# Attention values for all eight groups computed ahead of the group loop, row block 3 moved without DRAM, new orders

## The reference

```
xn = layernorm(x)
qkv = xn @ w_qkv.T                     # 32 query heads, 8 key and 8 value heads, 128 wide
scores = q k^T / sqrt(128), causal     # 4 query heads share one key/value head: 8 groups
attn = softmax(scores) @ v
s = attn @ w_dense.T                   # back to 512 features
g = silu(three +-1 matrix layers of xn, relu between, the last 20% of inputs times -4)
out = x + s * g
```

## Time and profile before

| | us |
|---|---|
| median of 3 runs | 915.27 (912.52 to 916.16) |
| profiled execution | 917.22 |
| its span, first to last instruction | 915.1 |
| PE busy | 896.1 (98%) |
| DVE, ACT, POOL busy | 677.7 (74%), 513.2 (56%), 463.3 (51%) |
| granted PE clock, mean | 0.997 |

### The profile page before, as it was taken

One profiled execution on the slowest core, in us unless ns is written; L12 is line 12 of the kernel. 1 busy time (PEld: TensorE's weight loads), 2 busy tenths in 40 slices (PEclk: granted clock), 3 DMA queues, 4 the chain that ended last, 5 costly groups with the idle time before them and its releaser, 6 DMA issues.

```text
span 915.1 us, 15937 instructions
## 1 busy us (share of the span) xinstructions
PE 896.1 (98%) x4272; PEld 757.4 (83%) x4272; DVE 677.7 (74%) x1163; ACT 513.2 (56%) x1077; POOL 463.3 (51%) x372
## 2 busy tenths in 40 slices
PE   7999999999999999999999999999999999999997
PEld 6878778888788878888788887888788887888886
DVE  7768767787677867788667876788677786678865
ACT  3656645665466645666356644666456663555633
POOL 5246443564346635555336634465445563355775
PEclk9999999999999999999999999999999999999999
DMA  6496655857386764865577573867549664655472
GB/s 218 121 249 192 132 115 156 241 132 152 66 239 197 155 120 115 244 165 118 103 192 222 136 155 61 243 185 153 109 127 255 157 124 86 171 151 125 103 202 86
DMA packets 204806, 143.58 MB, mean 157 GB/s; under 512 B 23152, under 2 KB 172144, under 8 KB 204784
## 3 DMA queue, kind: packets, MB, share of 16 engines
q1 hardware_dynamic: 176112, 129.68, 55.9%
q10 hardware_dynamic: 28672, 13.64, 6.9%
HBM read 63.70 MB, written 23.20 MB: 95 GB/s over the span
## 4 chain that ended last, share of the span: by engine, by line
issue 51%; POOL 30%; PE 14%; DMA 2%; SPq 1%; DVE 1%; POOLq 1%; ACT 0%; DVEq 0%
POOL pt_lo L767 21%; POOL w_lo L777 6%; POOL wd_lo L777 3%; PE ps_m L1251 3%; PE ps_s L1236 2%; PE ps_o L1119 1%; PE ps_o L1121 1%; PE ps_o L1120 1%; PE ps_m L1119 1%; PE ps_m L1120 1%; PE ps_m L1121 1%; PE ps_s L1120 1%; PE ps_s L1121 1%; PE ps_s L1119 1%; SPq L674 1%
## 5 line engine op out<-in xcount | busy, mean ns | idle before, releaser
L767 POOL TENSOR_TENSOR pt_lo<-pt_lo,pt_hi 128x512 fp32r<-128x512 f32 x248 | 326.2, 1339 | 257.6 <-ACT pt_hi L866 257.6
L959 DVE CUSTOM_DVE_ANT_0 ps_s<-ps_s,mask 128x32 f32<-128x32 f32 (+31 forms) x256 | 181.8, 716 | 93.7 <-PE ps_s L1121 92.2
L866 ACT ACTIVATE pt_hi<-pt_lo 128x512 fp32r<-128x512 f32 x288 | 172.6, 628 | 78.7 <-PE ps_o L1121 42.8
L1119 PE MATMUL ps_m<-xn_hi,w_hi 128*128 128x512 f32 (+1 forms) x388 | 152.2, 392 | 1.8 <-DVE q_lo L1067 1.8
L1121 PE MATMUL ps_m<-xn_hi,w_lo 128*128 128x512 f32 (+1 forms) x388 | 150.9, 389 | 0.0
L1120 PE MATMUL ps_m<-xn_lo,w_hi 128*128 128x512 f32 (+1 forms) x388 | 150.8, 389 | 0.0
L819 ACT ACTIVATE prob_even<-ps_s,small 128x32 f32<-128x32 f32 (+15 forms) x128 | 82.8, 648 | 99.5 <-DVE small L959 98.1
L819 ACT ACTIVATE prob_odd<-ps_s,small 128x160 f32<-128x160 f32 (+15 forms) x128 | 96.1, 754 | 63.1 <-DVE small L959 36.4
L1120 PE MATMUL ps_s<-k_lo,q_hi 128*128 128x480 f32 (+15 forms) x384 | 126.6, 330 | 0.0
L1121 PE MATMUL ps_s<-k_hi,q_lo 128*128 128x480 f32 (+15 forms) x384 | 126.5, 329 | 0.0
L1119 PE MATMUL ps_s<-k_hi,q_hi 128*128 128x480 f32 (+15 forms) x384 | 124.7, 325 | 0.0
(11 more groups left out here) (100 smaller groups left out, 1429.5 us busy)
## 6 DMA issues: line engine op xcount, KB each, us to landing
raw<-wqkv SPq DMA_DIRECT2D x48, 256.0 KB, 4.3
pt_lo<-prob_odd SPq DMA_DIRECT2D x96, 128.0 KB, 3.9
pt_lo<-prob_even SPq DMA_DIRECT2D x96, 112.0 KB, 3.2
pt_lo<-prob_odd SPq DMA_DIRECT2D x96, 96.0 KB, 2.7
raw<-wd SPq DMA_DIRECT2D x32, 256.0 KB, 4.1
inv_rows<-inv SPq DMA_DIRECT2D x32, 256.0 KB, 4.2
at_lo<-inv SPq DMA_DIRECT2D x32, 256.0 KB, 3.4
turned<-prob_odd SPq DMA_DIRECT2D x32, 256.0 KB, 4.1
```

Of the source, the lines that this page charges most:

```text
L767: pool.tensor_tensor(pt_lo[:, slot, :], pt_lo[:, slot, :].bitcast(F32), pt_hi[:, hi_slot, :], ALU.subtract).then_inc(land_lo, 1)
L866: act.activation(pt_hi[:, hi_slot, :], pt_lo[:, LAND_AT[i] + j, :].bitcast(F32), ACT.Copy).then_inc(land_hi, 1)
L959: dve.tensor_tensor_reduce(out=scores, in0=scores, in1=mask[:, S - width(i % BLOCKS, tile):S], scale=-1.0, scalar=BIG, op0=ALU.add, op1=AL ...
L1119: pe.matmul(out, sta_hi, mov_hi, start=start, stop=False)
```

## The change

The values of all groups are computed in the prologue, and laid the other way: a block of xn is the stationary operand, and the value weights of four groups (512 columns) are the moving one. `values.half.b` is one token block for groups 0 to 3 or 4 to 7: 12 matmuls, 16 such items. DVE copies the bank to one of four stages in `prob_even`, SP stores it to the DRAM tensor `values`. Value weights come in 8 loads to `y`, and are split by ACT and POOL into `wd_hi`/`wd_lo` and the upper 8 slots of `pt_lo`. In the body, `vload.h` reads four key blocks from DRAM, ACT and POOL split them; the v units, the copies to `vt` and `vblocks` are gone. Layernorm goes in four batches of two blocks. Row 3 is moved directly. RAW goes from 5 to 3, LAND from 12 to 16. The first unit of the prologue is no longer made in two column halves. A group's output weights are loaded at its own start. In `last`, feed-forward buffers and the waits for them follow the new layout. All lists are in a new order.

The diff, cut (BODY's lists in the parts that matter; `LAST` is changed in the same way; of the old lists the end of PE's is shown):

```diff
-RAW = 5
+RAW = 3
 HI_RING = 4
-LAND = 12
+LAND = 16
...
-BY_DRAM = 4
+BY_DRAM = 3
...
-PIECES = ["q0", "q1", "q2", "q3", "k", "v"]
+PIECES = ["q0", "q1", "q2", "q3", "k"]
+HALF_GROUPS = GROUPS // 2
+STAGES = 4
...
-LAND_AT = [0, 1, 3, 6, 1, 6, 0, 4]
+LAND_AT = [0, 6, 12, 8, 1, 10, 1, 8]
 COLUMNS = [list(range(i + 1)) for i in range(BLOCKS)]
 COLUMNS[6].reverse()
-LAND_AFTER = {0: tri(7), 2: 30 - PAIRS, 3: 34 - PAIRS, 4: tri(3), 5: tri(4), 6: tri(5) + 1, 7: tri(6) + 3}
+LAND_AFTER = {0: tri(1), 1: 23 - PAIRS, 2: 35 - PAIRS, 3: 32 - PAIRS, 4: tri(7) - PAIRS, 5: tri(4), 6: tri(5),
+              7: tri(6)}
...
+    values = lambda half, *blocks: [("values", half, b) for b in blocks]
-    pe = ln(0, 1, 2, 3) + unit("q0") + unit("q1") + unit("q2") + ln(4, 5) + unit("q3") + ln(6, 7) \
-        + unit("k") + unit("v") + [("scores", first, r) for r in tiles] + values
...
+    pe = ln(0, 1) + values(0, 0, 1) + ln(2, 3) + values(0, 2, 3) + unit("q0") + ln(4, 5) + unit("q1") \
+        + ln(6, 7) + unit("q2") + unit("q3") + unit("k") + values(0, 4, 5, 6, 7) \
+        + [("scores", first, r) for r in tiles] + values(1, *blocks)
+    q0, q1, q2, q3, k = [("unit", p, 0) for p in PIECES]
+    wv = [[("wv", half, c) for c in range(CHUNKS)] for half in range(2)]
     split = [("split", p) for p in PIECES]
...
+    root = [("root", n) for n in range(BATCHES)]
+    act = hi(wv[0][0]) + root[:1] + hi(*wv[0][1:], *ln(0, 1)) + root[1:2] + hi(split[0], *ln(2, 3), split[1]) \
+        + root[2:3] + hi(split[2], *ln(4, 5), q0, split[3]) + root[3:] \
+        + hi(*ln(6, 7), q1, split[4], q2, *wv[1][:2], q3, *wv[1][2:], k)
+    act += [("exp", first, r) for r in tiles] + hi(("vload", 0))
+    stats, scale = ([[(name, b) for b in blocks[n:n + 2]] for n in blocks[::2]] for name in ("stats", "scale"))
+    moments = [("moments", n) for n in range(BATCHES)]
+    dve = stats[0] + moments[:1] + scale[0] + lo(*ln(0, 1)) + stats[1] + moments[1:2] + scale[1] \
+        + lo(*values(0, 0), *ln(2, 3), *values(0, 1)) + stats[2] + moments[2:3] + lo(*values(0, 2)) + scale[2] \
+        + lo(*values(0, 3), *ln(4, 5), q0) + stats[3] + moments[3:] + scale[3] \
+        + lo(*ln(6, 7), q1, q2, q3, k, *values(0, 4, 5, 6, 7))
+    dve += [("max", first, r) for r in tiles] + lo(*values(1, 0)) + [("flip", first), ("inverse", first)] \
+        + lo(*values(1, *blocks[1:])) + [("ffn_scales",)]
+    pool = lo(*wv[0], *split, *wv[1]) + [("zero_y",), ("zero_odd",)] + lo(("vload", 0))
+    x = [("x", b) for b in blocks]
+    load = [("load", p) for p in PIECES]
+    wv_load = [[("wv_load", half, c) for c in range(CHUNKS)] for half in range(2)]
+    store = [[("store", half, b) for b in blocks] for half in range(2)]
+    sp = x[0:2] + wv_load[0] + x[2:4] + load[0:2] + x[4:6] + load[2:3] + x[6:8] + wv_load[1] \
+        + store[0][0:2] + load[3:4] + store[0][2:4] + load[4:5] + store[0][4:] \
+        + [("scales",), ("vload", 0), ("dw", first), ("rw", first)] + store[1][0:2] \
+        + [("dr", first), ("rr", first)] + store[1][2:]
...
 BODY = {
     "pe": """
-        scores.7.3 dense.3.1 weigh.5.2 dense.3.2 dense.3.3 unit.q1.0.0 weigh.5.3 unit.q1.0.1
-        weigh.5.4 unit.q1.0.2 weigh.5.5 weigh.6.6 unit.q1.0.3 weigh.6.5 weigh.6.4 weigh.6.3
-        unit.k.0.0 unit.k.0.1 weigh.6.2 unit.k.0.2 unit.k.0.3 dense.4.0 dense.4.1 dense.4.2
-        dense.4.3 weigh.6.1 unit.v.0.0 unit.v.0.1 scores.8.0 unit.v.0.2 unit.v.0.3 weigh.6.0
-        dense.5.0 scores.8.1 dense.5.1 dense.5.2 weigh.7.0 weigh.7.1 dense.5.3 weigh.7.2 weigh.7.3
-        weigh.7.4 vblocks.0 scores.8.2 weigh.7.5 weigh.7.6 weigh.7.7 scores.8.3 dense.6.0
-        dense.6.1 dense.6.2 dense.6.3 dense.7.0 dense.7.1 dense.7.2 dense.7.3
...
+        unit.q3.1.0 scores.1.0 scores.1.1 scores.1.2 scores.1.3 unit.q3.1.1 scores.2.0 unit.q3.1.2
+        unit.q3.1.3 scores.2.1 scores.2.2 unit.q0.1.0 scores.2.3 scores.3.0 unit.q0.1.1
+        unit.q0.1.2 weigh.0.0 scores.3.1 scores.3.2 unit.q0.1.3 unit.q1.1.0 scores.3.3 unit.q1.1.1
+        unit.q1.1.2 unit.q1.1.3 unit.q2.1.0 unit.q2.1.1 unit.q2.1.2 unit.q2.1.3 unit.k.1.0
+        unit.k.1.1 unit.k.1.2 unit.k.1.3 unit.q0.0.0 unit.q0.0.1 unit.q0.0.2 unit.q0.0.3
+        scores.4.0 scores.4.1 dense.0.0 weigh.1.0 dense.0.1 weigh.1.1 scores.4.2 scores.4.3
+        dense.0.2 dense.0.3 unit.q3.0.0 scores.5.0 scores.5.1 unit.q3.0.1 unit.q3.0.2 unit.q3.0.3
+        dense.1.0 weigh.2.0 scores.5.2 weigh.2.1 weigh.2.2 dense.1.1 scores.5.3 dense.1.2
+        weigh.3.0 weigh.3.1 dense.1.3 scores.6.0 weigh.3.2 weigh.3.3 dense.2.0 scores.6.1
+        dense.2.1 scores.6.2 dense.2.2 dense.2.3 unit.q1.0.0 weigh.4.0 scores.6.3 weigh.4.1
+        scores.7.0 weigh.4.2 weigh.4.3 scores.7.1 unit.q1.0.1 unit.q1.0.2 scores.7.2 unit.q1.0.3
+        weigh.4.4 scores.7.3 weigh.5.0 weigh.5.1 weigh.5.2 dense.3.0 dense.3.1 dense.3.2 weigh.5.3
+        weigh.5.4 dense.3.3 unit.q2.0.0 weigh.5.5 unit.q2.0.1 unit.q2.0.2 unit.q2.0.3 unit.k.0.0
+        unit.k.0.1 weigh.6.6 unit.k.0.2 unit.k.0.3 weigh.6.5 dense.4.0 dense.4.1 dense.4.2
+        weigh.6.4 scores.8.0 weigh.6.3 weigh.6.2 weigh.6.1 dense.4.3 dense.5.0 dense.5.1 dense.5.2
+        weigh.6.0 weigh.7.0 weigh.7.1 scores.8.1 dense.5.3 weigh.7.2 scores.8.2 weigh.7.3
+        scores.8.3 weigh.7.4 weigh.7.5 weigh.7.6 weigh.7.7 dense.6.0 dense.6.1 dense.6.2 dense.6.3
+        dense.7.0 dense.7.1 dense.7.2 dense.7.3
...
     "act": """
+        hi.land.5.1 hi.land.5.2 exp.7.1 hi.unit.q1.0 hi.land.5.3 amove.6.0 amove.6.1 hi.land.5.4
+        hi.land.5.5 amove.6.2 amove.6.3 hi.weigh.4 exp.7.2 exp.7.3 amove.7.0 hi.land.6.6
+        hi.land.6.5 hi.unit.q2.0 hi.land.6.4 hi.land.6.3 hi.land.6.2 hi.weigh.5 hi.unit.k.0
+        hi.land.6.1 amove.7.1 amove.7.2 amove.7.3 hi.land.6.0 exp.8.0 hi.land.7.0 hi.land.7.1
+        hi.land.7.2 hi.land.7.3 hi.land.7.4 hi.land.7.5 hi.weigh.6 hi.land.7.6 hi.land.7.7 exp.8.1
+        exp.8.2 exp.8.3 hi.weigh.7 hi.vload.0
...
     "dve": """
+        flip.6.1 flip.6.2 lo.unit.q1.0 flip.6.3 mul.weigh.4 max.7.2 max.7.3 lo.weigh.4 inverse.6
+        lo.dense.3 flip.7.0 flip.7.1 flip.7.2 mul.weigh.5 lo.unit.q2.0 lo.land.6.4 flip.7.3
+        lo.unit.k.0 lo.land.6.1 lo.weigh.5 inverse.7 max.8.0 lo.dense.4 lo.land.7.1 mul.weigh.6
+        lo.land.7.4 lo.dense.5 lo.weigh.6 max.8.1 lo.land.7.7 max.8.2 max.8.3 mul.weigh.7 flip.8
+        inverse.8 lo.weigh.7 lo.dense.6 lo.dense.7
...
     "sp": """
+        load.wd0 load.wd1 load.wd2 vload.1 dw.1 rw.1 load.wd3 load.q0 dr.1 load.q1 rr.1 dw.2
+        load.q2 load.q3 move.3.0 move.3.1 dr.2 move.3.2 move.3.3 rw.2 rw.3 load.k rr.2 move.4.0
+        move.4.1 move.4.2 move.4.3 rr.3 rw.4 move.5.0 move.5.1 rr.4 move.5.2 move.5.3 rw.5
+        move.6.0 move.6.1 move.6.2 move.6.3 rr.5 rw.6 move.7.0 move.7.1 move.7.2 rr.6 move.7.3
+        rw.7 rr.7 vload.0 dw.8 rw.8 dr.8 rr.8
...
+        def wv_parts(half, c):
+            if half == 0:
+                return wd_hi[:, c, :], wd_lo[:, c, :]
+            return pt_lo[:, LAND - 2 * CHUNKS + c, :], pt_lo[:, LAND - CHUNKS + c, :]
...
+        def stage(half, b):
+            slot = value_no(half, b) % STAGES
+            return prob_even[:, slot * E:(slot + 1) * E]
...
+                    elif what == "wv_load":
+                        n = wv_no(*item)
+                        sp.dma_start(y[:, n, :], wv_d[item[0], item[1], :, :]).then_inc(wv_loaded[n], 16)
+                    elif what == "store":
+                        half, b = item
+                        sp.wait_ge(shared_read, r.shared_no(("values", half, b)))
+                        groups = slice(half * HALF_GROUPS, (half + 1) * HALF_GROUPS)
+                        sp.dma_start(values_d[groups, :, b, :].rearrange("g t d -> t g d"),
+                                     stage(half, b).rearrange("t (g d) -> t g d", d=P))\
+                          .then_inc(values_stored[value_no(half, b) % STAGES], 16)
+                    elif what == "vload":
+                        half, = item
+                        ahead = 1 - half
+                        for stored_part in values_stored:
+                            sp.wait_ge(stored_part, 16 * BLOCKS // STAGES * (1 if kind == "prologue" else 2))
+                        if kind != "prologue":
+                            sp.wait_ge(block_weighed, WEIGHED0 + PAIRS * g + (PAIRS - HALF // P) * ahead)
+                        keys = slice(half * HALF // P, (half + 1) * HALF // P)
+                        src = values_d[bass.ds(g + ahead, 1), :, keys, :].rearrange("a t b d -> (a t) b d")
+                        sp.dma_start(v_lo[:, keys, :].bitcast(F32), src).then_inc(values_loaded[half], 16)
...
+                            if BY_DRAM <= i < BY_DRAM + 2:
+                                sp.wait_ge(landed[i % 2], LANDED0[i % 2] + r.landings(i - 2))
...
+                    elif what == "lo" and item[0][0] == "wv":
+                        _, half, c = item[0]
+                        hi, lo = wv_parts(half, c)
```

(45 more changed lines are left out.)

370 lines of the change are left out of this document (161 added, 209 removed).

## The result

The changed kernel takes 932.87 us (median; 929.49 to 934.65), the kernel before 915.12 (912.52 to 916.16): ratio 1.0194, 95% interval 1.0158 to 1.0230. It is slower, by some 18 us; the forecast was 907. The profiled execution took 933.09 us.

A forecast was written before the change was run, and what follows sets the result against it. PE's own work was taken to bound the body. Prologue 77.3, body 696.6 and last group 132.7 summed to 906.6 against the span of 915.1, -8.5 us; from the median 915.3 that gave 907, range 895 to 917.

The forecast's parts named there:

- Work of PE: Whole kernel: value products stay 192 matmuls; the 16 vblocks go, 0.44 us each, 7.0 us in all.
- weigh.7.0: Body: row 7's chain of 15.1 us fits under 15.3 us of PE items, so the 1.0 us stall goes.
- weigh.6.6: Body: row 6's chain needs 13.9 us, PE has 12.9; 1.0 us a group added, bounds 0 and 2.
- dense.7.0: Body: split of row 7 takes 3.6 us against PE's 3.4; 0.2 us of stall a group.
- Prologue: Before the groups: start 11.7, work 61.1, stalls 1.1 and 3.2, clock 0.2; 77.3 us against 35.26.
- ln.6: Prologue: DVE needs 5.9 us while PE has only unit q1, 2.72; 3.2 us stall, bounds 0 and 4.5.
- ln.0: Prologue's first work: starts at 9.7 us, before 11.78, with one port wait for each of two steps; bounds 8.6 and 11.8.
- Last group: Last group: 135.9 less one v unit and one vblocks, 132.7 us; the chain behind PE's end stays.
- rival 4: Body: SP, with a ring of 3, falls behind before move.3.0; 3 us a group, 928, slower; chance 0.07.
- Rival 2: Body: one more late item, 1 us a group, where an ACT copy waits behind an amove; 914; chance 0.18.
- Rival 3: Prologue: each of POOL's splits holds up DVE's moments and scales through the shared port; 912; chance 0.06.
- Rival 1: Lists hide every chain: no stall at ln.6, weigh.6.6 or dense.7.0; 894; chance 0.24.

The follow-up runs named there:

- e1_row7: Changed kernel with two body orders altered: DVE does flip.7.3 ahead of mul.weigh.5, SP issues rr.6 behind move.7.3; 924.14 us.
- e1b_row7_act: e1_row7 plus ACT issuing amove.7.1 to 7.3 earlier, between the splits of row block 6; 923.13 us.
- e13_weigh44: e9_pe with one edit: PE does weigh.4.4 ahead of scores.7.1, DVE's list unchanged; 900.17 us.
- e3_port: Changed kernel with one wait more: POOL starts splitting value weights only when the second row block is scaled; 928.11 us.
- e11_early: e9_pe with PE's weigh.4.4 ahead of scores.7.1 and DVE's max.7.2 and flip.7.0 earlier; 897.81 us, ratio to before 0.9809.
- e8_all: Changed kernel with e1b_row7_act, e2_last_sp, e3_port, earlier prologue statistics to scale of row blocks 6 and 7, and ACT's root before the first value-weight split; 909.32 us.
- e9_pe: e8_all with two PE items moved: unit.k.0.2 ahead of weigh.6.6 and dense.5.3 ahead of weigh.7.0; 909.86 us.
- e14_body: Changed kernel with only the landing-chain edits of the body, e1b_row7_act and both of e11_early; 913.64 us, ratio to before 0.9976.
- e2_last_sp: Changed kernel with SP's last-group order altered: vload.1, dw.1 and rw.1 ahead of load.wd3 and load.k0; 928.18 us, median of three executions.

## Why the prediction was wrong

- *Work of PE*: right. 6.8 us of transposes, forecast as 7.0; the values' work moved to the prologue, 16 items of 2.72 us from start to start.
- *weigh.7.0*: this step failed, and with it the sign. The prediction took the old length of the chain, 15.1 us from the item that frees the slots to weigh.7.0, and set it against 15.3 us of PE's items. In groups 1 to 6 the chain took 18.1 us (weigh.5.5 at 70.3 us, weigh.7.0 at 88.4), 2.8 more than before. With the 1.0 us at weigh.6.6 PE had 16.3 for it, and stood 1.9 us a group where none was forecast. By the issues and landings of the traces the 2.8 us are four parts. The first issue came 1.6 us after the start of weigh.5.5, against 0.9 after weigh.6.4, since flip.7.0 stood behind the eviction of dense.3 (0.7). Flip.7.3 and rr.6 were late (1.0, `e1_row7`), and so were the amoves (0.6, `e1b_row7_act`); the sentence that the 1.0 us at weigh.6.6 "covers" them was not worked out. And the moves were issued into a queue in which row 6 was still landing (73.1), where it had landed 6 us ahead of them before (72.0, 78.2): with flip and amoves mended the row still took 12.9 us from first issue to last landing, against 12.3 (0.6), and it took 11.9 once row 6 was out of the way (`e13_weigh44`). Forecast for the body 696.6, measured 712.2; some 3 us of this is the lower clock behind these waits (two groups of 102.8 and 103.2 us against 101.0 to 101.7).
- *weigh.6.6*: right, 1.0 us a group forecast, 0.99 measured; the chain from weigh.4.4, summed as 13.9 us, took 13.8.
- *dense.7.0*: under 0.1 us a group, not 0.2.
- *Prologue*: 77.3 forecast, 82.2 measured. ln.6 (3.2 against 3.15) and values(0,2) (1.1 against 1.36) were right. ln.0 came at 11.57 and not 9.7: the root ended at 8.14 (7.9 forecast), but from there it took 3.4 us, of which the hold-up by GpSimd was 2.0 (1.39 without it, `e3_port`); my 1.8 us had room for a fifth of that, though the text says one wait for each of the two steps. The rest, some 2.8 us, is PE at the 1.2 GHz level after each of the two stands (values(0,0) took 4.3 us and not 2.7, the first unit behind ln.6 3.6 and not 2.7, ln.6 itself 0.9 and not 0.4), for which I had taken 0.2.
- *Last group*: 132.7 forecast, 137.0 measured. Its rival stood in the text in the wrong place: SP did fall behind through the ring of 3, not at move.3.0 of the body but at load.k0 of the last group. I never walked SP's list of the last group.
- *The rivals*: rival 4 had the sign and, for the last group, the mechanism, not the price; in the body SP came to move.3.0 at 20.2 us and PE to weigh.3.0 at 41.1, so there it is out. Rival 2 had ACT's copies late behind the amoves; it was the amoves that were late behind the copies, and 0.6 us a group. Rival 3's port cost about 2 us in the prologue (`e3_port`). Rival 1 is not what the changed kernel did, but what `e11_early` reaches with its lists edited: its waits are 13.9 us in all, below the 21.6 of before, and 897.8 is near the 894 that it gave.
- *The signs of being wrong* that the prediction named both came: a group above 101 us (101.9) and a prologue above 80 (82.2).
- That `e8_all`, with its lists mended, comes to 909.3, near the 907, is partly luck: its prologue is 3 us shorter than forecast (74.3), its seven groups 5 us longer (701.6).

## What to carry to other kernels

When an edit lets a transfer start earlier, its old length holds only for the old conditions: price it again with the items that now stand ahead of each of its steps, and with the bytes that are still in flight ahead of it. Walk the chain piece by piece (slot freed, flip, issue, landing, split), through the lists of every engine and of every stage: here single items in the lists of PE, DVE, ACT and SP were in the wrong place, worth 1 to 10 us each, while a move of filler in front of a wait (`e9_pe`) was worth nothing. A change that loses can still be the better ground: with its landing chain mended this one is level with the kernel before or 0.2% faster (`e14_body`), and with prologue and last group mended too 1.9% faster (`e11_early`). Such edits of DVE and SP alone gained nothing on the old kernel; what its best orders would give is not known.

## What the hardware showed

- What limits the landing of a row here is bytes, not issues: in the windows of row 7 above the DMA engines are busy 0.96 to 1.04 of the time, at 178 to 203 GB/s. In `e1_row7` its pieces of 128 KB landed one in 0.6 to 0.7 us while SP alone issued, one each 0.65 us, and at the same pace when ACT's three issues joined, but for the very last (1.3 us). The last piece took 5.3 us from its issue in the changed kernel (366.50 to 371.85), where the first pieces of row 6 in `e13_weigh44`, of 112 KB, took 2.3.
- Under GpSimd's split of 128x512 (1.28 us) DVE steps on 2 columns took 1.13 to 1.27 us in place of 0.16 to 0.17. DVE's 128x512 statistics were not held up (two in 1.28 us under four splits). The Trainium skill ("SBUF — State Buffer", Who interferes with whom) says that an instruction with one SBUF input outside the 2-port modes does not contend; the statistics agree, and the one-input step of 1.20 us would have to be in such a mode, which no row shows.
- A value split, put ahead of the first root on ACT, brought a second table load of 1.28 us ahead of that root (6.65 us); with the root first, before and in `e8_all`, there is none between the one at 0.81 and the root.
- A wait of about 2 us at weigh.7.0 was followed by the 1.2 GHz level in two of seven groups of the changed kernel's profile, and cost these groups about 1.7 us more each. It need not be: in the profile of `e2_last_sp`, with the same waits in the body, the mean granted clock was 1.000, as in `e11_early` without them.
